# Second layer's last recurrence sums, projection, normalisation and router moved to later tiles, and the expert weights loaded in one run at attention's end

## What is computed

```python
h = layernorm(x) * (1 + ca) + sa
x = x + ga * softmax_attention(h)              # 16 heads of 8
h = layernorm(x) * (1 + cb) + sb
x = x + gb * moe64(h)                          # top 8 of 64 in 4 of 8 groups, silu(x Wg) * (x Wu) Wd, plus 2 shared
h = layernorm(x) * (1 + ca) + sa
# second block's attention: a step for each of its positions
#   (the 16 sequences are the steps, the 256 tokens its batch)
v_bar = einsum("bhvk,bhk->bhv", W, k_i)
W = W + einsum("bhv,bhk->bhvk", b_i * (v_i - v_bar), k_i)
y = einsum("bhvk,bhk->bhv", W, q_i)            # W is 8 x 16 for each head and token
x = x + ga * (y @ Wo + bo)
h = layernorm(x) * (1 + cb) + sb
x = x + gb * moe8(h)                           # softmax router over 9, top 2, gelu(x w1) w2, the ninth passes h on
```

## Time and profile before

| | us |
|---|---|
| median of three executions | 1828.72 |
| lowest and highest | 1826.63, 1829.84 |
| the profiled execution | 1828.58 |
| its span, first to last instruction | 1826.5 |
| setup and attention in the span | 0 to 391.6 |
| first mixture, eight chunks | 391.6 to about 1377 |
| one loop iteration of it (DVE's last addition to the state, 891.52 to 1012.69) | 121.2 |
| second mixture, eight chunks | about 1377 to the end |

### The profile page before, as it was taken

The page is one execution under the profiler, slowest core; times in us unless marked ns, Lnnn a source line. Parts: engine busy times, 40 slices in busy tenths (PEclk is TensorE's granted clock), DMA queues, the critical chain, the costliest instruction groups (busy, mean ns, idle before and its releaser), DMA issues.

```text
span 1826.5 us, 25499 instructions
## 1 busy us (share of the span) xinstructions
PE 1659.0 (91%) x7212; PEld 1027.0 (56%) x7212; DVE 1366.2 (75%) x2636; ACT 819.6 (45%) x1533; POOL 691.8 (38%) x628
## 2 busy tenths in 40 slices
PE   3888888869989999999999999999998899899999
PEld 2455555446655656556665565655655555555555
DVE  4777777656979988979969889799698587544444
ACT  1566767657644234243352342533525543433333
POOL 2011111100002945928739469187394475000000
PEclk9989989989999999999999999999999999999999
DMA  6554445246575877677767666666671111111110
GB/s 199 152 157 129 119 111 152 89 125 215 180 207 188 222 205 204 210 209 214 215 189 203 187 188 197 189 197 204 190 194 52 41 47 52 35 57 53 52 52 23
DMA packets 172698, 269.49 MB, mean 148 GB/s; under 512 B 23748, under 2 KB 61981, under 8 KB 170053
## 3 DMA queue, kind: packets, MB, share of 16 engines
q1 hardware_dynamic: 168691, 266.33, 49.9%
q10 hardware_dynamic: 1874, 1.36, 0.2%
q0 software_dynamic: 2048, 0.79, 0.2%
HBM read 233.78 MB, written 34.62 MB: 147 GB/s over the span
## 4 chain that ended last, share of the span: by engine, by line
PE 36%; DVE 16%; issue 10%; POOL 10%; ACT 3%; DMA 3%; SPq 1%; DVEq 0%; POOLq 0%; ACTq 0%
PE psum L1528 10%; PE psum L1368 6%; POOL e_prod L1986 6%; PE psum L1370 6%; PE psum L1369 6%; PE psum L1383 5%; DVE psum L1897 4%; POOL e_phi L1986 3%; DVE e_hm L1900 2%; DVE e_vbar L1755 2%; DVE e_y L1755 1%; DVE e_state L1850 1%; DMA e_ring<-w_split 1%; PE psum L1462 1%; DMA rw<-rw_fm 1%
## 5 line engine op out<-in xcount | busy, mean ns | idle before, releaser
L1694 ACT ACTIVATE e_gu<-psum 128x512 f32<-128x512 f32 (+1 forms) x368 | 219.3, 598 | 545.5 <-PE psum L1370 284.3
L1368 PE MATMUL psum<-e_hhi,e_ring 128*128 128x512 f32 x704 | 434.0, 616 | 19.7 <-DMA e_ring<-w_split 11.5
L1383 PE MATMUL psum<-e_hm,w_d 128*128 128x512 f32 (+1 forms) x736 | 382.6, 601 | 15.0 <-DVE e_hm L1903 7.2
L1986 POOL TENSOR_TENSOR e_prod<-e_state,e_phi 128x512 f32<-128x512 f32 x256 | 353.4, 1417 | 2.4 <-POOL e_phi L1986 1.7
L1897 DVE TENSOR_TENSOR psum<-psum,rw 128x512 f32<-128x512 f32 x352 | 243.4, 692 | 90.9 <-PE psum L1370 85.1
L1935 DVE TENSOR_TENSOR e_hm<-psum,rw 128x512 f32<-128x512 f32 x256 | 174.6, 688 | 178.0 <-ACT psum L1722 176.9
L1369 PE MATMUL psum<-e_hhi,e_ring 128*128 128x512 f32 x704 | 279.0, 396 | 0.0
L1370 PE MATMUL psum<-e_hlo,e_ring 128*128 128x512 f32 x704 | 278.8, 396 | 0.0
L1900 DVE TENSOR_TENSOR e_hm<-psum,e_gu 128x512 f32<-128x512 f32 x352 | 243.5, 692 | 39.4 <-ACT e_gu L1694 15.7
L1528 PE MATMUL psum<-e_hm,w_gu 128*128 128x512 f32 x512 | 262.9, 598 | 6.6 <-DVE w_d L1916 5.5
L1722 ACT ACTIVATE psum<-psum 128x512 f32<-128x512 f32 x256 | 148.8, 582 | 254.7 <-PE psum L1370 238.8
(11 more groups left out here) (304 smaller groups left out, 2181.0 us busy)
## 6 DMA issues: line engine op xcount, KB each, us to landing
e_ring<-w_split SPq DMA_DIRECT2D x308, 256.0 KB, 4.2
rw<-rw_fm SPq DMA_DIRECT2D x192, 176.0 KB
qk_parts<-at_part SPq DMA_DIRECT2D x96, 192.0 KB, 3.1
rw<-gates_fm SPq DMA_DIRECT2D x72, 256.0 KB, 3.2
w_split<-e_ring SPq DMA_DIRECT2D x44, 256.0 KB, 2.7
rw<-rw_fm SPq DMA_DIRECT2D x64, 160.0 KB
at_qs<-qk_parts SPq DMA_DIRECT2D x16, 576.0 KB
at_ks<-qk_parts SPq DMA_DIRECT2D x16, 576.0 KB
```

Of the source, the lines that this page charges most:

```text
L1368: pe.matmul(out, w_hi, x_hi, start=first, stop=False)
L1383: mm = pe.matmul(ps[:, ACC, :], weights_at(T, WD + P * j, P)[0:rows(j), :], hm[0:rows(j), slot(j), :], start=(j == 0), stop=(j == HT - 1))
L1694: a(act_g[0:r, j % 2, :], ps[0:r, GB[j % 2], :], ACT.Silu).then_inc(silu_done, 1)
L1986: ins = tt(out[:, at], x[:, at], y[:, at], op)
```

## The change

Two independent edits. The first takes `load_weights` out of the rounds and puts all 16 behind them. The second moves slots in the part "b" of `jobs`; no instruction of it is added or taken away.

| step of part "b" | engine | slot before | slot now |
|---|---|---|---|
| last four sums of y | DVE | 2, 3, 5, 6 | 3, 5, 7, 9 |
| transposes of y, copy | PE, ACT | 9 | 12 |
| output projection | PE | 11 | 14 |
| new x (`xb`) | DVE | 12 | 15 |
| `pe_x`, copy of x, statistics | PE, ACT, DVE | 13 | 16 |
| standard deviation | ACT | 15 | 18 |
| `dve_norm` | DVE | 16 | 19 |
| `pe_n`, scaled h | PE, ACT | 19 | 21 |
| logits | PE | 21 | 23 |
| router: maximum, exp, gates, rank, cut | DVE, ACT | 22, 23, 24, 25, 28 | 24, 25, 26, 27, 30 |
| transposes of the gates, copy | PE, ACT | 34 | 36 |

```diff
-PIECE_ROUNDS = (0, 1, 2, 3, 13, 14, 15, 16)
...
-                if k in PIECE_ROUNDS:
-                    for i in range(2):
-                        load_weights(2 * PIECE_ROUNDS.index(k) + i)
 
             run(sp, iteration)
+            for half in range(2):
+                sp.wait_ge(nrows_in[half], 16 * BATCH)
+            for piece in range(WEIGHT_PIECES):
+                load_weights(piece)
+                load_weights(WEIGHT_PIECES + piece)
...
-        Y_LAST = {2: (1, 0, 0), 3: (1, 0, 1), 5: (1, 1, 0), 6: (1, 1, 1)}
+        Y_LAST = {3: (1, 0, 0), 5: (1, 0, 1), 7: (1, 1, 0), 9: (1, 1, 1)}
...
-                    if j == 13:
+                    if j == 16:
                         pe.wait_ge(xb_done, m + 1)
                         ln_b.pe_x(pe)
-                    if j == 19:
+                    if j == 21:
                         ln_b.pe_n(pe, m)
...
-                    if j == 16:
+                    if j == 19:
                         ln_b.dve_norm(dve, m)
-                    if j == 22:
+                    if j == 24:
                         dve.wait_ge(lg1_done, m + 1)
                         held["router"] = router(m)
```

More of the change, by code:

```diff
@@ L1482, in jobs @@
                     m = c - 2
-                    if j == 9:
+                    if j == 12:
                         if k > 2:
@@ L1492, in jobs @@
                         mm.then_inc(yt_done, 1)
-                    if j == 11:
+                    if j == 14:
                         pe.wait_ge(yfm_done, m + 1)
                         pe.matmul(side_b, wo[:], y_fm[:], start=True, stop=True).then_inc(wo_done, 1)
-                    if j == 13:
+                    if j == 16:
                         pe.wait_ge(xb_done, m + 1)
                         ln_b.pe_x(pe)
-                    if j == 19:
+                    if j == 21:
                         ln_b.pe_n(pe, m)
-                    if j == 21:
+                    if j == 23:
                         pe.wait_ge(ln_b.h, m + 1)
@@ L1506, in jobs @@
                         mm.then_inc(lg1_done, 1)
-                    if j == 34:
+                    if j == 36:
                         pe.wait_ge(cut, m + 1)
@@ L1665, in jobs @@
                         a(y_fm, side_b, ACT.Copy).then_inc(yfm_done, 1)
-                    if j == 13:
+                    if j == 16:
                         act.wait_ge(xb_done, m + 1)
                         a(cols(x_fm, m), xb, ACT.Copy).then_inc(xb_kept, 1)
-                    if j == 15:
+                    if j == 18:
                         ln_b.act_std(act, m)
-                    if j == 19:
+                    if j == 21:
                         ln_b.act_h(act, m)
@@ L1677, in jobs @@
                         ins.then_inc(h1_kept, 1)
-                    if j == 23:
+                    if j == 25:
                         act.wait_ge(shifted, m + 1)
                         a(pr[:], w0[:], ACT.Exp).then_inc(exp_done, 1)
-                    if j == 34:
+                    if j == 36:
                         act.wait_ge(g1t_done, m + 1)
@@ L1859, in jobs @@
                         y_sum(m, *Y_LAST[j])
-                    if j == 12:
+                    if j == 15:
                         dve.wait_ge(wo_done, m + 1)
@@ L1872, in jobs @@
                         ins.then_inc(xb_done, 1)
-                    if j == 13:
+                    if j == 16:
                         ln_b.dve_stats(dve, m)
-                    if j == 16:
+                    if j == 19:
                         ln_b.dve_norm(dve, m)
-                    if j == 22:
+                    if j == 24:
                         dve.wait_ge(lg1_done, m + 1)
                         held["router"] = router(m)
-                    if j == 24:
+                    if j == 26:
                         router_gates(m, held["router"])
-                    if j == 25:
+                    if j == 27:
                         router_rank(held["router"])
-                    if j == 28:
+                    if j == 30:
                         router_cut(held["router"])
```

## The result

The changed kernel takes 1854.36 us in the median of four executions (1847.32 to 1856.51), beside 1829.28 us (1826.63 to 1832.92) for the kernel before. The ratio is 1.0126, 95% interval 1.0101 to 1.0152: slower by 1.3%, as forecast (1853 us). The profiled execution took 1852.48 us with a span of 1850.7 us, 24.2 us more than before.

| part of the span | before | after | difference |
|---|---|---|---|
| to the addition of chunk 1 | 647.42 | 641.00 | -6.4 |
| six iterations of the first mixture's loop | 732.80 | 766.36 | +33.6 |
| from there to the end | 446.28 | 443.34 | -2.9 |

The account below looks back on a forecast made before the run. PE, busy 91% of the span, was taken as the bound, with DVE and POOL nearly closing the loop too. 1828.6 - 8 (weights) + 24 (slots) + 8.5 (clock) = 1853 us, range 1836 to about 1868.

Parts of the forecast that it names:

- (a): `pe_x` behind `xb`, slot 16: PE waits 2.4 us instead of 1.5, +0.9 us an iteration.
- (b): ACT's sigmoid and square root no longer meet in slot 15, -0.8 us; sums of y lighten DVE's first tiles, -0.3.
- (c): `pe_n` behind `dve_norm`, slot 21: PE newly waits 3.6 us an iteration, as DVE has crowded slots 18 and 19.
- (d): Slots 24 to 31: the router's first part joins DVE's sums of v and additions, +0.8 us an iteration.
- (e): End of the iteration: DVE's 0.95 us wait for POOL becomes slack, up to -0.4 us.
- the first rival: First mixture's loop: POOL sets it and PE's wait costs nothing; 1815 us, faster; chance 0.10.
- (f): PE's clock falls behind the longer stalls, one low stretch in five of six iterations: +8.5 us, bounds 0 and 20.
- The rival of two falls in an iteration: First mixture's loop: the clock falls after both stalls; 1864 us; no separate chance, forecast with either clock course 0.74.
- Part 1: Attention: weights behind the rounds shrink PE's stalls in rounds 1 and 15; net -8 us, bounds -12 and -3.
- The rival of a store that waits for the weights: End of attention: 16 loads at half speed, routing weights' store lands 12 us late; 1865 us; chance 0.08.
- The second mixture: Moved slots there: 0 us, bounds -2 and +2, as slots are 1.65 tiles apart or the keys' sums are gone.

Follow-up runs that it names:

- the later reader: Changed kernel, `xb` at DVE slot 14, `pe_n` at 22 in place of 21, router one slot later: 1799.73 us; with weights back in their old rounds: 1814.99 us.
- its last eight weights: Kernel before with only the weights of rounds 13 to 16 moved behind the rounds: 1824.09 us, ratio 0.9971.
- its short addition: Kernel before with DVE's addition to the state in slot 43 cut to the first head, the rest left out: 1818.73 us, ratio 0.9951.

## Why the prediction was right, step by step

To check the steps, an iteration of each kernel without disturbance in its front part and with at most one low stretch: PE's down projections in the slots 18, 21, 28 and 38, first before (its iteration starts at DVE's last addition at 1012.69 and ends at 1133.83), then after (1152.67 to 1278.79).

```profile
1061.15 1.02 PE L1383 MATMUL psum<-e_hm,w_d 128*128 128x512 f32 x2
...
1069.23 1.02 PE L1383 MATMUL psum<-e_hm,w_d 128*128 128x512 f32 x2
...
1084.96 1.02 PE L1383 MATMUL psum<-e_hm,w_d 128*128 128x512 f32 x2
...
1112.18 1.02 PE L1383 MATMUL psum<-e_hm,w_d 128*128 128x512 f32 x2
```

```profile
1201.17 1.02 PE L1384 MATMUL psum<-e_hm,w_d 128*128 128x512 f32 x2
...
1212.61 1.05 PE L1384 MATMUL psum<-e_hm,w_d 128*128 128x512 f32 x1
...
1230.11 1.02 PE L1384 MATMUL psum<-e_hm,w_d 128*128 128x512 f32 x2
...
1257.09 1.02 PE L1384 MATMUL psum<-e_hm,w_d 128*128 128x512 f32 x2
```

| stretch | before | after | difference | predicted |
|---|---|---|---|---|
| start to slot 18: (a), (b), sums of y | 48.46 | 48.50 | 0.0 | -0.2 |
| 18 to 21: (c), first half of the low stretch, logits gone | 8.08 | 11.44 | +3.4 | +3.6 |
| 21 to 28: second half of the low stretch, logits come | 15.73 | 17.50 | +1.8 | +1.7 |
| 28 to 38: (d) | 27.22 | 26.98 | -0.2 | +0.8 |
| 38 to the last addition: (e) | 21.65 | 21.70 | 0.0 | -0.4 |
| iteration | 121.14 | 126.12 | +5.0 | +5.5 |

Single rows of this table hide two things that cancel: the logits moved from slot 21 to 23 (0.9 us of PE), and the low stretch begins with the transposes of slot 21. So the stall and the clock are told apart in another iteration: with the slots alone there is one (from 781.39) whose stall of 3.31 us has no low stretch behind it. Its rows for slot 18, the transposes of slot 21 and slot 28:

```profile
833.36 1.02 PE L1383 MATMUL psum<-e_hm,w_d 128*128 128x512 f32 x2
...
842.87 0.66 PE L849 MATMUL psum<-ident,e_nt 128*128 128x128 f32 x4 [3.31 <-DVE e_nt L828]
...
860.69 1.02 PE L1383 MATMUL psum<-e_hm,w_d 128*128 128x512 f32 x2
```

From slot 18 to slot 28 it takes 27.3 us, beside 23.8 before and 28.9 in the changed kernel: 3.5 us for the stall and what goes with it, and 1.6 us for the low clock.

- **(a), (b).** The wait for `xb` grew from 1.5 to 2.30 us (predicted 2.4), and the three terms nearly cancel as they should. The tile from slot 17 to 18, 3.05 us before (1058.10 to 1061.15), takes 2.24 now (1198.93 to 1201.17), which is the 0.8 us put down to ACT's tables. ACT has three table loads of 1.28 us in that place before (the prediction counted two for each function) and twice two in separate slots now. No run moved them alone, so that cause is argued, not shown.
- **(c)** decided, and the sum holds piece by piece: the tile's pair begins 950.50 - 948.75 = 1.75 us behind the down projection (1.84), PE's transposes come 958.25 - 948.75 = 9.50 us behind it (9.7), and PE was ready 9.50 - 3.31 = 6.2 us behind it (6.1). Moving either end by a slot removed the wait or cut it by a tile's 2.25 us.
- **(d)** was mis-sized. The step took the router's first part at 1.23 us from a row in which it met POOL's products. Where it lands now POOL stands still, and it takes 973.69 - 973.05 = 0.64 us (DVE's next multiplication after the router's start); the gates' product in line 1776 also shrank, from 0.94 to 0.42 us. 1.2 - 0.6 - 0.5 is nothing, as measured. The step's rule, that DVE's time in these slots reaches PE, held where the router was moved to slot 23: 1.1 us an iteration. What it had wrong is the duration, which it took as fixed.
- **(e)** failed. The wait of 0.95 us was read as POOL's chain being late and should have become slack. It is the same 0.95 us in five of the six iterations of both kernels (the last has none), since it is made by DVE's own addition in slot 43. That also removes the ground of the first rival: POOL is no bound of its own; in the changed kernel it waited 60.1 us for DVE's sums of v, 23.2 before.
- **(f)** was set too low: nine low stretches of 1.6 us, about 14 us where 8.5 stood, less 1.1 us by which the two stretches of before lengthened theirs. The rival of two falls in an iteration came true in three of the six. That these stretches pass on in full is borne out by the kernel with `xb` in 14: from slot 28 to slot 38 PE takes 26.8 us and from there to the last addition 21.9, with a low stretch behind the stall (from 1007.01) as without one (from 1130.20).
- **The loop:** the iteration of the table is 5.0 us longer with one low stretch, so 3.4 without. 6 x 3.4 + 9 x 1.6 - 1.1 = 33.7 us, and 33.6 were measured. The step had 24 + 8.5 = 32.5 us: the waits came out lower than forecast (20 for 24) and the clock higher (13 for 8.5), so that the sum is nearer than its terms, and this is luck. The split weights (15.0 us of waits over the span, 11.5 before) have no share in it: in the loop PE waited about 9 us for them in either kernel.
- **Part 1:** -8.9 us at ACT's start for -8 predicted, -7 to -10 by the ratios. The store of the routing weights landed in 3.0 instead of 2.3 us, and ACT started 382.73 - 356.62 = 26.1 us behind POOL's last issue against 25.5: the half microsecond predicted. The rival of a store that waits for the weights is out. Of the gain in attention 2.5 us were given back by the addition of chunk 1.
- **The second mixture** was put at 0, with bounds of 2 us, and the part behind the loop is 2.9 us shorter (it is the same 443.4 us with the slots alone). One wait of 2.43 us for the normalised tile is new there (1597.35). What shortened the part in spite of it was not tried. This term and part 1 miss in opposite directions, another reason why the total fits so well.

## What to carry to other kernels

In a loop that PE fills to nine tenths, the distance in slots between a writer and its reader is what a moved job has to keep; count what the writer's engine has queued ahead of it in its new slot, since each of the two distances that were one slot short cost some 21 us here. Such a wait can be mended at either end. Look at what else moves with each: here the later reader also took small operations out of the way of another engine's long ones. And read a wait for an engine back one step further: the engine named may only be late because the waiting one held it up.

## What the hardware showed that was not expected

- A DVE operation with two inputs in SBUF and POOL's products exclude each other both ways: 128x2048 on DVE (2.90 us) makes POOL's product 6.93 instead of 4.15 us, and POOL's pieces make a 128x36 operation on DVE take 0.87 to 0.96 instead of 0.18 to 0.22 us. The sums (one input, 1.21 us) keep their length beside POOL's products.
- In a loop in which PE is otherwise busy, the clock fell behind stalls of 3.3 to 3.45 us fifteen times in 18 and behind stalls of 2.3 to 2.4 us seven times in 18 (the changed kernel, its slots alone, and those with one stall mended), and behind none of the 36 stalls of 1.0 to 1.5 us (the kernel before, its weights alone, its last eight weights, its short addition, and the two with the later reader alone). Each fall of 3.4 us behind a stall cost 1.3 to 1.8 us, mostly 1.6 (one lasted 6.8 us and cost 2.8). The clock also fell in places without such a stall, as at 857.1 before, so a stall is not its only occasion.
